# A GpSimd wait for the split row maxima, and a channel sum placed behind a gate remainder, in a four-block kernel on one core

## The chip, the cores and the metric

The kernel runs on one core of a Trainium2 chip. The metric is the device time of one execution in microseconds (us), the median of several runs. The engines are TensorE (PE in the profile; its weight loads are PEld), VectorE (DVE), ScalarE (ACT), GpSimd (POOL) and SyncE (SP, whose queue issues the DMAs). They run side by side, each its own instructions strictly in order, and wait for one another through semaphores.

## The reference, cut to what matters

Input x is 16 sequences of 512 tokens and 128 channels, fp32. Four blocks follow one another, each with a residual and a layer norm:

```
x = _layernorm(x + _L0_attn_ref(x, ...))   # time mix with a decaying sum, then channel mix
x = _layernorm(x + _L0_ffn_ref(x, ...))    # soft decision tree, depth 8
x = _layernorm(x + _L1_attn_ref(x, ...))   # causal attention, 16 heads of 8
x = _layernorm(x + _L1_ffn_ref(x, ...))    # 16 experts, the best 2 by softmax, plus 2 shared

# time mix:
k = exp(min(xk @ Wk, 60)); v = xv @ Wv; r = xr @ Wr
wk, wkv = _wkv(k, k * v, decay, first)     # running sums over the tokens
rwkv = sigmoid(r) * (wkv / (wk + 1e-8))
x = x + rwkv @ Wo
# channel mix:
kv = silu(xk @ cm_Wk) @ cm_Wv
x = x + (sigmoid(xr @ cm_Wr) + kv)
# attention: weights = softmax(causal scores)
# experts: g = softmax(u @ centroids.T + bias), kept for the 2 largest of 16
```

## The kernel before, in words

One sequence (a "batch" in the code, b = 0 to 15) goes through all four blocks as a [128 x 512] tile set. The work of five consecutive batches is interleaved. `run` (in `build`) counts turns; a table `ORDER` gives for each engine a list of tokens such as `1:gated0`, and in turn t the token `lag:step` runs that step for batch t - lag, if there is such a batch. So a list is the exact order of an engine's instructions, written out by hand. In the middle of the run every turn does one batch's worth of everything: lag 0 and 1 are the time and channel mix, lag 1 and 2 the tree and the making of q and k, lag 2 and 3 the attention, lag 3 and 4 the experts.

Semaphores count finished steps. `until(engine, b, name, n)` lets the engine wait until step `name` of batch b has been signalled n times (all its times if n is left out), and does nothing for a negative b.

The 512 hidden channels of the time mix are four chunks, c = 0 to 3. The steps that matter here, with their lines:

- `wk0` (L381, GpSimd): the first term is added to the decaying key sum of chunk 0. [128 x 512]
- `inverse0` (L675, VectorE): its reciprocal.
- `r_sig0` (L385, GpSimd): the sigmoid, from a tanh that ScalarE has made.
- `gated0` (L390, GpSimd): sigmoid times the decaying key-value sum of chunk 0. [128 x 512], both inputs in SBUF.
- `rwkv0` (L395, GpSimd): gated0 times inverse0. It needs both.
- `u15` (L436, GpSimd): the input of expert 15, of the batch that is three behind the time mix's; TensorE's `expert15` (L905, `wexpT`) needs it. GpSimd's list has it directly behind `gated0`.
- `max_parts` (L733, L638, L737, L739, VectorE): the row maxima of the attention scores, [128 x 64], are negated and split into three bf16 parts, by four small instructions, each of which waits for the one before. They signal `max_part` four times. TensorE's `maxT` (L905, `max_cols`) transposes the parts; its list goes on with experts 12 to 15, then `r2` and the scores (L905, `qh,kh`), which have the maxima as extra rows by way of a ScalarE copy and a DMA.
- `cmr_sig` (L403, GpSimd) and `cmr_sum` (L408, GpSimd): the channel mix's gate, and the gate plus the residual, [128 x 512].
- `y0` (L694, VectorE): that sum plus the channel mix's matmul. It needs `cmr_sum` and all of `cmv_ps`. Behind it VectorE's list has row maxima 8 and 9 and the statistics of y0, and TensorE's `xnT` waits for it.
- `largest0`, `others`, `largest1`, `gates` (L784 to L802, VectorE): the choice of two experts by small [128 x 64] instructions; `others` is the one that writes `left`.
- `gate_hi` and `gate_mid` (L488, ScalarE), `gate_rest` (L426, GpSimd) and `gate_lo` (L430, GpSimd): the gates split into three bf16 parts. gate_rest needs gate_hi, gate_mid needs gate_rest, gate_lo needs gate_mid. TensorE's `gT` needs gate_hi and gate_lo.

`max_parts` is at lag 3 in VectorE's list and `gated0` at lag 1 in GpSimd's, so in one turn they belong to batches two apart. In GpSimd's list `gated0` stands after `r_sig0` and `wk0`, and in VectorE's list `wkv0`, which it needs, stands eight steps ahead of `max_parts`.

Of the kernel before, what the change touches and what calls it, by code (L numbers as in the profile page):

```python
# [53 lines left out]
    pool="""  # L54
        4:u3 4:u5 4:u7 4:u9 4:u11 4:u13 1:r_sig0 1:wk0 1:gated0 4:u15 1:r_sig1 1:rwkv0 4:root7 1:wk1 1:gated1 0:root0 2:root_rms 1:r_sig2 1:gated2 1:rwkv1
        1:wk2 2:root4 1:wk3 2:rope_sum0 1:r_sig3 2:rope_sum1 2:rest0 1:gated3 1:rwkv2 1:rwkv3 2:part_lo0 2:rest1 2:part_lo1 1:res 1:root2 0:x1_gain
        0:x1_bias 0:root1 3:root6 1:cmr_sig 1:cmr_sum 3:gate_rest 3:gate_lo 1:root3 3:u1
    """,
    act="""
        4:route_exp 2:cmk_tanh3 2:cmr_tanh 1:norm1 4:gate_hi 4:gate_mid 1:mix_before0 4:gT_out 1:mix_before1 1:mix_before2 4:spread1 2:norm3 4:spread3  # L60
# [33 lines left out]
def build(nc: bass.Bass, a, out):  # L94
    with ExitStack() as ctx:
        def sb(name, shape, dt=F32):
            return ctx.enter_context(nc.sbuf_tensor(name, shape, dt))
# [6 lines left out]
        def raised(ins, name, by=1):  # L104
            ins.then_inc(sems[name], by)

        def until(eng, b, name, n=None):

            per = PER_BATCH[name]
            if b >= 0:  # L110
                eng.wait_ge(sems[name], b * per + (per if n is None else n))
# [74 lines left out]
        max_part, gate_part = (t[:, 0:J * PARTS * NH].rearrange("p (j i h) -> p j i h", j=J, i=PARTS) for t in (max_cols, gate_cols))  # L186
# [12 lines left out]
        gate_rest = sb("gate_rest", [P, J, NE])  # L199
# [135 lines left out]
        def _(pool):  # L335
# [51 lines left out]
            def gated(b, c):  # L387
                until(pool, b, "r_sig", c + 1)
                until(pool, b, "wkv", c + 1)
                raised(pool.tensor_tensor(rth[:, c % 2, :], rth[:, c % 2, :], kvb[:, c % 2, :], ALU.mult), "gated")  # L390

            def weighted(b, c):
# [39 lines left out]
            def gated_input(b, e):  # L432
# [5 lines left out]
            pool_steps = {  # L438
                **{f"root{n}": (lambda b, n=n: root(b, n)) for n in LNS}, "root_rms": root_rms, "x1_gain": first_gain, "x1_bias": first_bias,
                **each("wk", C, weight_sum), **each("r_sig", C, receptance), **each("gated", C, gated), **each("rwkv", C, weighted),  # L440
                "res": residual, "cmr_sig": channel_gate, "cmr_sum": channel_sum,
                **each("rope_sum", 2, rope_sum), **each("rest", 2, first_rest), **each("part_lo", 2, third_part),
# [794 lines left out]
```

How the kernel before makes its waits and increments, by code:

```python
        def until(eng, b, name, n=None):  # L107
            per = PER_BATCH[name]
            if b >= 0:
                eng.wait_ge(sems[name], b * per + (per if n is None else n))
# [1 line left out]
        def reached(eng, name, total):  # L113
            if total > 0:
                eng.wait_ge(sems[name], total)
# [177 lines left out]
        @block.sync  # L294
# [21 lines left out]
                until(sp, b, "out_ready")  # L316
                sp.dma_start(out[b].rearrange("(j p) h -> p j h", p=P), yo[:, :, :]).then_inc(sems["stored"], 16)
            load(0)
            for dst, src in GAINS:
                sp.dma_start(dst, src, allow_slow_non_contiguous=True).then_inc(setup["gains_in"], 16)
            for dst, src in FIRST[0::2]:
                sp.dma_start(dst, src, allow_slow_non_contiguous=True).then_inc(setup["first_loaded"], 16)
            for dst, src in LOADS[ON_ACT:]:
                sp.dma_start(dst, src, allow_slow_non_contiguous=True).then_inc(setup["loaded"], 16)
            sp.wait_ge(setup["bias_parts"], 7)
            for i in range(PARTS):
                sp.dma_start(bias_rows[i:i + 1, :], bias_part[i]).then_inc(setup["bias_in"], 16)
            sp.wait_ge(setup["kh_ones"], 4)
# [4 lines left out]
        @block.gpsimd  # L334
# [110 lines left out]
            ones_of_heads(0)  # L445
            ones_of_heads(1)
            pool.wait_ge(setup["constants"], 4)
            pool_steps["root0"](0)
            ones_of_heads(2)
            pool.wait_ge(setup["gains_in"], ALL_GAINS)
            pool_steps["x1_gain"](0)
            pool_steps["x1_bias"](0)
```

## Time and profile before

| | |
|---|---|
| median of 3 runs | 1956.96 us (1956.66 to 1959.65) |
| the profiled execution, own time | 1953.77 us |
| its span, first to last instruction | 1951.9 us |
| busy: PE, DVE | 1677.3 us (86%), 1554.8 us (80%) |
| busy: ACT, POOL | 1009.0 us (52%), 889.5 us (46%) |
| mean granted TensorE clock | 0.962 |
| chain that ended last, by engine | PE 49%, DVE 33%, POOL 6%, ACT 5% |

The span holds 20 turns, of which the 13 from turn 4 to turn 16 have all five batches in work; each of these takes about 110 us. "Busy" counts an instruction's time on its engine, waiting for the memory included. The chain is followed back from the last instruction, at each step to what released it. TensorE and VectorE take turns in bounding the program, so each stretch has to be read by itself.

### The profile page before, as it was taken

What the parts mean: (1) busy time and instruction counts of PE and PEld (TensorE: products, weight loads), DVE (VectorE), ACT (ScalarE), POOL (GpSimd) and SP (SyncE); (2) the same over time, 40 slices, a digit from 0 to 9 for tenths busy, and PEclk for the clock granted to TensorE, in tenths of its full rate; (3) what the DMA queues carried; (4) which work ended last, traced back from release to release, by engine and by line L of the source; (5) the groups of instructions that cost most, each with busy time, mean ns of one, the idle gap of its engine ahead of it and who ended that gap; (6) DMA issues with size and microseconds to landing.
All of it is one profiled execution on the core that took longest, in us unless ns stands there. A gap on an engine that the chain in (4) does not pass through costs nothing.

```text
span 1951.9 us, 34254 instructions
## 1 busy us (share of the span) xinstructions
PE 1677.3 (86%) x12161; PEld 1088.7 (56%) x12269; DVE 1554.8 (80%) x3386; ACT 1009.0 (52%) x1998; POOL 889.5 (46%) x1120
## 2 busy tenths in 40 slices
PE   3466898999899998999998998999998998988876
PEld 1234456565656656565655656565665656565634
DVE  4676879798897979798897979799897979793712
ACT  3233463737455463737556473836556473726152
POOL 4544253736355463727355463726345363622202
PEclk9687899999999999999999999999999999999897
DMA  3001010100102010100102010110102020100100
GB/s 98 0 6 54 2 53 5 45 16 18 45 3 60 2 55 7 38 24 14 49 2 60 2 55 8 33 29 10 53 2 61 2 55 1 31 26 22 35 7 6
DMA packets 66924, 53.39 MB, mean 27 GB/s; under 512 B 8322, under 2 KB 65474, under 8 KB 66754
## 3 DMA queue, kind: packets, MB, share of 16 engines
q1 hardware_dynamic: 63202, 49.55, 9.2%
q8 instruction: 98, 1.61, 0.4%
q10 hardware_dynamic: 3552, 1.65, 0.3%
q14 instruction: 72, 0.59, 0.1%
HBM read 8.44 MB, written 4.19 MB: 6 GB/s over the span
## 4 chain that ended last, share of the span: by engine, by line
PE 49%; DVE 33%; POOL 6%; ACT 5%; issue 5%; SPq 1%; DMA 0%; ACTq 0%; DVEq 0%; POOLq 0%; another core or an unknown queue 0%
PE bank L905 47%; DVE rmax L728 10%; PE bank L901 3%; DVE prob L808 3%; DVE stats L629 3%; ACT prob L488 2%; DVE rmax L725 2%; DVE mixed L638 2%; POOL rstd L351 2%; ACT xd L494 1%; DVE mv L634 1%; DVE kvsum L667 1%; SPq L325 1%; DVE left L638 1%; POOL x L399 1%
## 5 line engine op out<-in xcount | busy, mean ns | idle before, releaser
L488 ACT ACTIVATE prob<-bank 128x512 f32<-128x512 f32 x640 | 357.4, 597 | 95.5 <-PE bank L905 88.4
L728 DVE TENSOR_REDUCE rmax<-bank 128x1 f32<-128x512 f32 (+2 forms) x768 | 353.7, 502 | 14.6 <-PE bank L905 13.1
L436 POOL TENSOR_TENSOR prob<-xdT,spread 128x512 f32<-128x512 f32 x128 | 162.2, 1267 | 354.6 <-ACT spread L488 354.6
L905 PE MATMUL bank<-kh,qh 72*128 72x512 bf16 (+3 forms) x1024 | 266.6, 308 | 45.2 <-DVE rmax L728 36.3
L905 PE MATMUL bank<-wexpT,prob 128*128 128x128 f32 x2048 | 278.1, 284 | 0.8 <-POOL prob L436 0.6
L905 PE MATMUL bank<-qh,kh 75*128 75x512 bf16 (+3 forms) x1024 | 256.5, 304 | 20.6 <-ACT prob L488 17.8
L905 PEld LDWEIGHTS bank<-wexpT,prob 128*128 128x128 f32 x2048 | 259.9, 198 | 19.0 <-issue 12.5
L488 ACT ACTIVATE spread<-bank 128x512 f32<-128x512 f32 x128 | 76.4, 597 | 338.2 <-PE bank L905 330.1
L905 PEld LDWEIGHTS bank<-qh,kh 75*128 75x128 bf16 x1024 | 100.1, 98 | 206.9 <-ACT prob L488 138.2
L675 DVE RECIPROCAL wkb<-wkb 128x512 f32<-128x512 f32 x64 | 211.5, 3325 | 0.0
L905 PE MATMUL bank<-maskb,identb 128*128 128x128 bf16 x1024 | 194.4, 223 | 0.0
L905 PE MATMUL bank<-maskTb,identb 128*128 128x128 bf16 x1024 | 193.3, 221 | 0.0
L905 PEld LDWEIGHTS bank<-kh,qh 72*128 72x128 bf16 x1024 | 101.6, 99 | 143.5 <-DVE rmax L728 93.2
L905 PE MATMUL bank<-prob,vaug 128*32 128x512 f32 (+3 forms) x2048 | 176.2, 445 | 3.0 <-ACT prob L488 2.9
L347 POOL TENSOR_TENSOR var<-mv,eps_ln 128x4 f32<-128x4 f32 x112 | 27.7, 247 | 230.8 <-DVE mv L634 230.2
L905 PEld LDWEIGHTS bank<-maskb,identb 128*128 128x128 bf16 x1024 | 102.4, 100 | 39.0 <-issue 23.5
L381 POOL TENSOR_TENSOR wkb<-wkb,ksum 128x512 f32<-128x512 f32 x64 | 93.6, 1463 | 64.7 <-DVE ksum L662 56.5
L905 PEld LDWEIGHTS bank<-maskTb,identb 128*128 128x128 bf16 x1024 | 101.3, 99 | 24.2 <-issue 22.6
L351 POOL TENSOR_TENSOR rstd<-var,exponent 128x4 f32<-128x4 f32 x112 | 113.8, 1016 | 1.2
L488 ACT ACTIVATE rth<-bank 128x512 f32<-128x512 f32 x128 | 75.4, 589 | 68.4 <-PE bank L905 60.8
L395 POOL TENSOR_TENSOR inner<-rth,wkb 128x512 f32<-128x512 f32 x64 | 82.4, 1287 | 56.9 <-DVE wkb L675 55.3
L808 DVE TENSOR_TENSOR prob<-xdT,bank 128x512 f32<-128x512 f32 x128 | 86.9, 679 | 26.0 <-PE bank L905 22.4
(211 smaller groups left out, 3447.3 us busy)
## 6 DMA issues: line engine op xcount, KB each, us to landing
qh<-part SPq DMA_DIRECT2D x288, 64.0 KB
kh<-part SPq DMA_DIRECT2D x288, 64.0 KB
x<-in_L_attn_x_dram SPq DMA_DIRECT2D x16, 256.0 KB, 2.8
out_dram<-yo SPq DMA_DIRECT2D x16, 256.0 KB, 2.4
qh<-maxT SPq DMA_DIRECT2D x16, 48.0 KB
wk<-in_L_attn_tm_Wk_dram ACTq DMA_DIRECT2D x1, 256.0 KB
wv<-in_L_attn_tm_Wv_dram ACTq DMA_DIRECT2D x1, 256.0 KB
wr<-in_L_attn_tm_Wr_dram ACTq DMA_DIRECT2D x1, 256.0 KB
```

Of the source, the lines that this page charges most:

```text
L351: raised(pool.tensor_tensor(rstd[:, n, :], var[:, n, :], exponent[:, :], ALU.pow), f"root{n}")
L381: raised(pool.tensor_tensor(wkb[:, c % 2, :], wkb[:, c % 2, :], ksum[:, c % 2, 0:T], ALU.add), "wk")
L395: raised(pool.tensor_tensor(inner[:, c, :], rth[:, c % 2, :], wkb[:, c % 2, :], ALU.mult), "rwkv")
L436: raised(pool.tensor_tensor(ug[:, e % 4, :], xdT[:, :], spread[e // 2 % 2][:, :], ALU.mult), "ug_side")
L488: raised(act.activation(dst, src, func, **kw), signal)
L629: last = dve.bn_stats(stats[:, n, j, :], t[:, j, :])
L638: return dve.scalar_tensor_tensor(out=out_, in0=in0, scalar=scalar, in1=in1, op0=op0, op1=op1)
L675: raised(dve.reciprocal(wkb[:, c % 2, :], wkb[:, c % 2, :]), "wk_inv")
L728: last = dve.tensor_reduce(rmax[:, j, h:h + 1], S[n % 2][:, col:col + (j + 1) * P], AX_X, ALU.max)
L808: raised(dve.tensor_tensor(ug[:, e % 4, :], xdT[:, :], G, ALU.mult), "ug")
L901: last = pe.transpose(bk[:, j * P:(j + 1) * P], t[:, j, :], ident[:, :])
L905: return pe.matmul(out_, w, x, start=start, stop=stop, **kw)
```

## The change

Two edits. GpSimd's `gated0` of batch b additionally waits until `max_parts` of batch b - 2 has signalled all four times, which is the `max_parts` of the same turn. And GpSimd's list has `gate_rest` ahead of `cmr_sum` instead of behind it. No instruction is added or removed, and no other engine's list changes.

```diff
@@ -54,7 +54,7 @@
     pool="""
...
-        0:x1_bias 0:root1 3:root6 1:cmr_sig 1:cmr_sum 3:gate_rest 3:gate_lo 1:root3 3:u1
+        0:x1_bias 0:root1 3:root6 1:cmr_sig 3:gate_rest 1:cmr_sum 3:gate_lo 1:root3 3:u1
     """,
@@ -387,6 +387,8 @@
             def gated(b, c):
                 until(pool, b, "r_sig", c + 1)
                 until(pool, b, "wkv", c + 1)
+                if c == 0:
+                    until(pool, b - 2, "max_part")
                 raised(pool.tensor_tensor(rth[:, c % 2, :], rth[:, c % 2, :], kvb[:, c % 2, :], ALU.mult), "gated")
```

The first place, on GpSimd around `gated0` in a turn of the middle (`prob<-xdT,spread` are the experts' inputs, the last of them u15), before:

```order
L436 TENSOR_TENSOR prob<-xdT,spread 128x512 [waits s_expert_ps,s_spread_out] x5
L385 TENSOR_SCALAR rth<-rth 128x512 [waits s_r_tanh]
L381 TENSOR_TENSOR wkb<-wkb,ksum 128x512 [waits s_k_sum,s_k_first]
L390 TENSOR_TENSOR rth<-rth,kvb 128x512 [waits s_wkv,s_r_sig]
L436 TENSOR_TENSOR prob<-xdT,spread 128x512 [waits s_expert_ps,s_spread_out]
L385 TENSOR_SCALAR rth<-rth 128x512 [waits s_r_tanh]
L395 TENSOR_TENSOR inner<-rth,wkb 128x512 [waits s_wk_inv,s_gated]
```

The same place of the changed kernel:

```order
L438 TENSOR_TENSOR prob<-xdT,spread 128x512 [waits s_expert_ps,s_spread_out] x5
L385 TENSOR_SCALAR rth<-rth 128x512 [waits s_r_tanh]
L381 TENSOR_TENSOR wkb<-wkb,ksum 128x512 [waits s_k_sum,s_k_first]
L392 TENSOR_TENSOR rth<-rth,kvb 128x512 [waits s_max_part,s_wkv,s_r_sig]
L438 TENSOR_TENSOR prob<-xdT,spread 128x512 [waits s_expert_ps,s_spread_out]
L385 TENSOR_SCALAR rth<-rth 128x512 [waits s_r_tanh]
L397 TENSOR_TENSOR inner<-rth,wkb 128x512 [waits s_wk_inv,s_gated]
```

The order is the same (lines behind the edit read two higher); the product of `gated0` has one more semaphore to wait for, and u15, r_sig1 and rwkv0 are queued behind it.

The second place, on GpSimd between the gate of the channel mix and the last part of the expert gates, before:

```order
L355 TENSOR_TENSOR shift<-minus,rstd 128x4 [waits s_root6]
L403 TENSOR_SCALAR thr<-thr 128x512 [waits s_cmr_tanh]
L408 TENSOR_TENSOR thr<-thr,x_0 128x512 [waits s_res,s_cmr_sig]
L426 TENSOR_TENSOR gate_rest<-gts,gate_cols 128x64 [waits s_gate_hi]
L430 TENSOR_TENSOR gate_cols<-gate_rest,gate_cols 128x4x16 [waits s_gate_mid]
```

The same place of the changed kernel:

```order
L355 TENSOR_TENSOR shift<-minus,rstd 128x4 [waits s_root6]
L405 TENSOR_SCALAR thr<-thr 128x512 [waits s_cmr_tanh]
L428 TENSOR_TENSOR gate_rest<-gts,gate_cols 128x64 [waits s_gate_hi]
L410 TENSOR_TENSOR thr<-thr,x_0 128x512 [waits s_res,s_cmr_sig]
L432 TENSOR_TENSOR gate_cols<-gate_rest,gate_cols 128x4x16 [waits s_gate_mid]
```

The channel sum now stands behind the gates' remainder, and so behind the wait for ScalarE's gate_hi.

## Rows read from the trace of the kernel before

**Rows 1.** Chain that ended last, us 659.6 to 673, shares by line

```profile
by line: PE bank L905 66.8%; DVE max_rest L638 9.1%; DVE max_cols L737 8.7%; DVE rmax L725 4.5%; ACT prob L488 4.5%; DVE max_cols L739 4.3%; DVE max_cols L733 3.4%; issue 1.9%; PE bank L901 0.9%; ACTq L111 0.1%
```

**Rows 2.** Timeline, DVE: start us, us, engine, line, instruction

```profile
659.66 0.45 DVE L733 TENSOR_SCALAR max_cols<-rmax 128x64 bf16<-128x64 f32 x1
660.15 1.22 DVE L638 SCALAR_TENSOR_TENSOR max_rest<-rmax,max_cols 128x64 f32<-128x64 f32 x1
661.40 1.16 DVE L737 CAST max_cols<-max_rest 128x64 bf16<-128x64 f32 x1
662.59 0.57 DVE L739 TENSOR_TENSOR max_cols<-max_rest,max_cols 128x64 bf16<-128x64 f32 x1
663.08 3.34 DVE L675 RECIPROCAL wkb<-wkb 128x512 f32<-128x512 f32 x1
```

**Rows 3.** Timeline, POOL, the same stretch (wk0, gated0, u15, r_sig1)

```profile
658.79 1.27 POOL L381 TENSOR_TENSOR wkb<-wkb,ksum 128x512 f32<-128x512 f32 x1
660.01 1.27 POOL L390 TENSOR_TENSOR rth<-rth,kvb 128x512 f32<-128x512 f32 x1
661.23 1.27 POOL L436 TENSOR_TENSOR prob<-xdT,spread 128x512 f32<-128x512 f32 x1
662.46 0.63 POOL L385 TENSOR_SCALAR rth<-rth 128x512 f32<-128x512 f32 x1
```

**Rows 4.** Timeline, PE, the same stretch; in brackets idle before, and releaser

```profile
659.32 1.02 PE L905 MATMUL bank<-mixed,wk 128*128 128x512 f32 x2
663.22 0.40 PE L905 MATMUL bank<-identb,max_cols 128*128 128x128 bf16 x4 [2.88 <-DVE max_cols L739]
663.45 3.79 PE L905 MATMUL bank<-wexpT,prob 128*128 128x128 f32 x32
```

**Rows 5.** Instructions on max_cols, DVE: duration ns min/median/max, first and last start

```profile
L733 DVE TENSOR_SCALAR max_cols<-rmax x16: 194/454/459, 219.6 to 1855.1; 128x64 bf16<-128x64 f32 x16
L638 DVE SCALAR_TENSOR_TENSOR max_rest<-rmax,max_cols x16: 224/1216/1218, 219.8 to 1855.3; 128x64 f32<-128x64 f32 x16
L737 DVE CAST max_cols<-max_rest x16: 194/1154/1156, 220.1 to 1855.6; 128x64 bf16<-128x64 f32 x16
L739 DVE TENSOR_TENSOR max_cols<-max_rest,max_cols x16: 225/570/1218, 220.3 to 1855.8; 128x64 bf16<-128x64 f32 x16
```

**Rows 6.** Timeline, DVE: the reciprocal of chunk 1, same turn

```profile
681.84 3.32 DVE L675 RECIPROCAL wkb<-wkb 128x512 f32<-128x512 f32 x1
```

**Rows 7.** Timeline, POOL: a gated product begun beside it

```profile
684.38 1.28 POOL L390 TENSOR_TENSOR rth<-rth,kvb 128x512 f32<-128x512 f32 x1
```

**Rows 8.** Windows of one turn: length, busy (x) by engine PE to POOL, clock, DMA

```profile
438.24:549.74 111.50, 102.17 (x759) 67.46 (x765) 96.65 (x210) 62.27 (x124) 54.71 (x69) 0.98 0.10 28
549.74:659.66 109.92, 100.58 (x759) 65.78 (x765) 96.67 (x209) 62.18 (x124) 54.69 (x69) 1.00 0.10 28
```

**Rows 9.** Windows, two us behind TensorE's wait for max_cols in that first turn

```profile
444.00:446.00 2.00, 2.00 (x11) 2.00 (x11) 2.00 (x3) 0.42 (x1) 0.85 (x1) 0.50 0.09 25
```

**Rows 10.** Timeline, PE: experts 12 to 15 in the turn of rows 9

```profile
442.03 5.42 PE L905 MATMUL bank<-wexpT,prob 128*128 128x128 f32 x32
```

**Rows 11.** Chain that ended last, us 727 to 757, shares by line

```profile
by line: DVE rmax L728 40.9%; DVE prob L808 10.2%; issue 8.8%; DVE rmax L725 6.0%; DVE stats L629 5.5%; DVE mixed L638 5.4%; DVE left L638 4.5%; DVE kvsum L667 3.8%; DVE hot L792 2.6%; DVE tree L638 2.6%; DVE mv L634 2.3%; DVE kvb L657 2.0%
```

**Rows 12.** Instructions on left: duration ns min/median/max, first and last start us

```profile
L638 DVE SCALAR_TENSOR_TENSOR left<-hot,pe_ x16: 224/1332/1335, 286.1 to 1914.3; 128x64 f32<-128x64 f32 x16
```

**Rows 13.** Timeline, DVE: the end of gates, and y0

```profile
730.82 0.22 DVE L802 TENSOR_TENSOR gts<-pe_,hots 128x64 f32<-128x64 f32 x1
...
731.56 0.68 DVE L694 TENSOR_TENSOR x<-thr,bank 128x512 f32<-128x512 f32 x1
```

**Rows 14.** Timeline, POOL: cmr_sum and gate_rest

```profile
727.35 1.27 POOL L408 TENSOR_TENSOR thr<-thr,x 128x512 f32<-128x512 f32 x1
731.41 0.30 POOL L426 TENSOR_TENSOR gate_rest<-gts,gate_cols 128x64 f32<-128x64 f32 x1 [2.79 <-ACT gate_cols L488]
```

**Rows 15.** Timeline, ACT: gate_hi

```profile
731.08 0.26 ACT L488 ACTIVATE gate_cols<-gts 128x64 bf16<-128x64 f32 x1 [2.98 <-DVE gts L802]
```

## The prediction

> **What bounds the kernel now.** I began with the shares of busy time: TensorE 86% and VectorE 80%, neither full, so the bound moves between them within a turn. The chain of waits then says where. Around the split of the row maxima [rows 1] two thirds of the chain are TensorE's matmuls, but a quarter is the four small VectorE instructions of max_parts (9.1 + 8.7 + 4.3 + 3.4%). TensorE stands still for 2.88 us until the last of them is done [rows 4]. Around the choice of experts and the 25 us behind it the chain lies on VectorE nearly throughout [rows 11]. So what shortens max_parts moves the end, and what delays y0 moves it too. GpSimd is on neither path by its own work.
>
> **How long max_parts has to take.** Its four pieces took 0.45, 1.22, 1.16 and 0.57 us, 659.66 to 663.16 [rows 2]: 3.50 us. The instructions by name show the same four at their fastest: 0.194, 0.224, 0.194 and 0.225 us [rows 5]. The slow ones end in step with GpSimd. The first ends at 660.11, as wk0 does (660.06); the second at 661.37, as gated0 does (661.28); the third at 662.56, as u15 does (662.50); the fourth at 663.16, as r_sig1 does (663.09) [rows 2, 3]. A VectorE piece that is issued while a GpSimd instruction runs is thus held until that one ends. Medians near the slow values say that this is the rule: it is so in turns 4 to 16, 13 of the 16. The first split, in turn 3, is undisturbed, and the last two are disturbed in their last piece alone, by u15, with no gated0 about.
>
> **Part one, the wait of gated0.** It takes gated0, u15 and r_sig1, all behind it in GpSimd's order, out of this stretch. wk0 stays.
> - The first piece still runs beside wk0. Its price lies between 0.20 us (free) and 0.46 us (held). I take 0.45, as now, since wk0 ends at 660.06 in either kernel.
> - The other three run free, with the 0.03 us between them that they have now: 660.15 to 660.37, 660.40 to 660.59, 660.62 to 660.85. The end comes 663.16 - 660.85 = 2.3 us earlier.
> - TensorE's previous matmul ends at 660.34 [rows 4], so it can follow: its idle time falls from 2.88 to about 0.6 us. It issues maxT at 660.91, then experts 12 to 15.
> - gated0 starts 0.07 us after the last piece, the time GpSimd takes from ScalarE's gate_hi (731.34) to gate_rest (731.41) [rows 14, 15]: 660.92. u15 begins 1.23 us later and ends at 663.4. TensorE wants it for the last quarter of the 3.65 us of experts: 660.91 + 0.23 + 2.74 = 663.9. It is in time by 0.4 us. r_sig1 ends at 664.0, and rwkv0 needs the reciprocal, which begins at 660.78 and ends at 664.1. So nothing queued behind the wait is late, and there is no GpSimd DMA among it. ScalarE, SyncE's maxima transfer and VectorE's next clamp hang on events that all move 2.3 us forward.
> - New neighbours: gated0 and u15 now run beside the reciprocal instead of beside the small pieces. Such a pair stands in the trace: a gated product of 1.28 us begins in the middle of a reciprocal of 3.32 us [rows 6, 7], and neither is longer than elsewhere (1.27 and 3.34). I cost it at nothing. By the Trainium skill (SBUF — State Buffer, "Who interferes with whom") VectorE and GpSimd share one pair of memory ports; whoever issues first keeps it for the whole instruction, and copy, cast and tensor_scalar can take it with a single SBUF input. The reciprocal is not in that list; were it treated like those, rival 2 would be what happens.
>
> Sum of part one: 13 turns x 2.3 = 29.9 us less.
>
> **The clock behind it.** In some turns TensorE's granted clock falls to 0.50, its 1.2 GHz level, directly behind the 2.88 us of standing still [rows 9], and experts 12 to 15 take 5.42 instead of 3.79 us [rows 4, 10]. Such a turn lasts 111.5 instead of 109.9 us [rows 8]; one turn of each kind is shown, and of the 13 four are of the slow kind. In the whole middle of the program the clock falls nowhere else. With 0.6 us of standing still I expect the four falls to go: 4 x 1.6 = 6.4 us less, with ends of 0 and 6.4.
>
> **Part two, the channel sum behind gate_rest.** cmr_sum, 727.35 to 728.62, now holds up the piece that writes left (1.33 instead of 0.22 us) [rows 12, 14]. Away from there it frees VectorE's choice of experts by 1.11 us. But VectorE then comes to y0, and y0 needs cmr_sum. Step by step: gates end at 731.04 - 1.11 = 729.93 [rows 13]; gate_hi starts 0.04 later and ends at 730.23; gate_rest runs 730.30 to 730.60; cmr_sum starts 0.04 before that end and takes 1.27: 731.83; y0 starts 0.05 later, at 731.88. Before, it started at 731.56. So VectorE gains 1.1 us, waits for all of it and 0.3 us more. gate_lo moves from 732.38 to about 732.1 and holds nobody. Since this stretch is VectorE's [rows 11], the 0.3 us counts, in the 14 turns (3 to 16) in which gates and channel sum meet: 4.5 us more. Its ends: 0, if TensorE's row maxima absorb it, and 14 x 0.6 = 8.4, if each handover costs a little more.
>
> **Sum.** 1953.8 (the profiled execution's own time; span 1951.9) - 29.9 - 6.4 + 4.5 = 1922.0 us. The median of the runs is 3.2 us above the profiled execution. If that is two more falls of the clock it goes as well, if not it stays: 1922 to 1925. I say 1923.
>
> **Rivals.**
> 1. *The clock still falls*, as often as now, elsewhere in the turn: TensorE would now stand about 1 us in one piece where it waits for y0. Then 1953.8 - 29.9 + 4.5 = 1928, 1931 by the median. Against it: all four falls followed the long wait. Chance 0.20. Experts kept waiting for u15 (its 0.4 us used up, say 0.2 us late) end in the same place: 13 x 0.2 = 2.6 us, 1926; within the forecast's range.
> 2. *The reciprocal holds up gated0 (slower).* It is issued at 660.78, before gated0. If GpSimd had to wait for its end at 664.1, u15 would end at 664.1 + 1.23 + 1.27 = 666.6, and expert 15, due at 663.9, would start 2.7 us late: more than the 2.3 us gained. 13 x 0.4 = 5 us more, the clock as now, and part two's 4.5: 1957.0 + 10 = 1967. It decides from 2.3 us of delay on. Rows 6 and 7 speak against it. Chance 0.03.
> 3. *The change doesn't do what it says:* the small pieces are slow for a reason of their own, and moving GpSimd frees none. Then part one gives 0 (the 0.6 us left of u15's and rwkv0's slack still cover it), and y0 waits for gate_rest at its old end, 731.71, plus 1.23 for the sum and 0.05: 732.99, 1.43 us late. 14 x 1.43 = 20 us: 1977. The undisturbed 0.2 us in turns without these neighbours [rows 5, 12] speak against it. Chance 0.03.
> 4. *Part two costs nothing* because VectorE makes good its 0.3 us behind y0, and the falls go too: 1918. Chance 0.12.
>
> **Numbers.** The forecast has 0.62, its own range 1919 to 1928. The range given reaches from just below rival 4 to rival 1 by the median, 1916 to 1932, and leaves out rivals 2 and 3 and the unforeseen. A difference of 0.2%, 3.9 us, is about what measurements of this kernel can tell from none. Faster by more than that: the forecast, rivals 1 and 4, 0.94; slower: rivals 2 and 3, with some chance that either is milder than worked out, 0.04; within: 0.02.
>
> **What would show it.** In the changed profile: pieces two to four of max_parts at 0.19 to 0.23 us in all 16 turns, the first still 0.45; TensorE's idle time ahead of maxT near 0.6 us; gated0 starting within 0.1 us behind the last piece; experts 12 to 15 at about 3.8 us without a gap, in every turn; turns of about 107.9 us; left at 0.22 us; VectorE idle for 1.4 us ahead of y0, released by GpSimd; y0 0.3 us later counted from the logits' first instruction. It would be wrong if VectorE's reciprocal or GpSimd's product grew beside each other, if TensorE waited for u15, or if the clock fell in more turns than four.

## The result, and the profile after

The changed kernel takes 1933.9 us (median of 4 runs, 1932.13 to 1935.45); the kernel before, on the same chip, 1957.07. The ratio is 0.9878 with a 95% interval of 0.9862 to 0.9893: 23 us faster. The forecast was 1923 with a range of 1916 to 1932, so the gain was a third smaller than said, and the time lies just outside the range. Of all the executions behind this document one, of the kernel with part one alone, took 4075 us; its ratio leaves it out.

The page of the changed kernel, busy time, and the chain that ended last:

```profile
PE 1684.5 (87%) x12161; PEld 1092.2 (57%) x12269; DVE 1512.3 (78%) x3386; ACT 1008.8 (52%) x1998; POOL 888.4 (46%) x1120
...
PE 53%; DVE 26%; POOL 7%; issue 7%; ACT 5%; SPq 1%; DMA 0%; DVEq 0%; ACTq 0%; POOLq 0%; another core or an unknown queue 0%
```

VectorE lost 42 us of "busy" time though it has the same 3386 instructions: that was time in which small instructions were held, 13 x 2.3 us in max_parts and 14 x 1.1 us in `left`, less 3 us by which the row maxima grew. Its share of the chain fell from 33% to 26%. TensorE's busy time grew by 7 us with the same instructions, which is the first sign of its clock.

**The first place.** Timelines of the changed kernel around max_parts, VectorE, GpSimd and TensorE:

```profile
653.87 0.46 DVE L735 TENSOR_SCALAR max_cols<-rmax 128x64 bf16<-128x64 f32 x1
654.36 0.23 DVE L640 SCALAR_TENSOR_TENSOR max_rest<-rmax,max_cols 128x64 f32<-128x64 f32 x1
654.62 0.20 DVE L739 CAST max_cols<-max_rest 128x64 bf16<-128x64 f32 x1
654.85 0.22 DVE L741 TENSOR_TENSOR max_cols<-max_rest,max_cols 128x64 bf16<-128x64 f32 x1
654.99 3.34 DVE L677 RECIPROCAL wkb<-wkb 128x512 f32<-128x512 f32 x1
...
655.25 1.27 POOL L392 TENSOR_TENSOR rth<-rth,kvb 128x512 f32<-128x512 f32 x1 [0.97 <-DVE max_cols L741]
656.47 1.27 POOL L438 TENSOR_TENSOR prob<-xdT,spread 128x512 f32<-128x512 f32 x1
...
655.13 0.40 PE L907 MATMUL bank<-identb,max_cols 128*128 128x128 bf16 x4 [0.58 <-DVE max_cols L741]
655.37 3.79 PE L907 MATMUL bank<-wexpT,prob 128*128 128x128 f32 x32
```

They answer to [rows 2 to 4]. Pieces two to four take what they take alone; all four need 1.20 us instead of 3.50. TensorE's standing still fell from 2.88 to 0.58 us. gated0 and u15 run beside the reciprocal, and neither is longer. The experts run through, 3.79 us.

**The second place.** VectorE's last gate instruction and y0, GpSimd's gate_rest and channel sum, and TensorE's xnT:

```profile
613.60 0.23 DVE L804 TENSOR_TENSOR gts<-pe_,hots 128x64 f32<-128x64 f32 x1
...
615.83 0.69 DVE L696 TENSOR_TENSOR x<-thr,bank 128x512 f32<-128x512 f32 x1 [1.40 <-POOL thr L410]
...
614.20 0.31 POOL L428 TENSOR_TENSOR gate_rest<-gts,gate_cols 128x64 f32<-128x64 f32 x1 [3.05 <-ACT gate_cols L490]
614.46 1.26 POOL L410 TENSOR_TENSOR thr<-thr,x 128x512 f32<-128x512 f32 x1
...
616.67 0.63 PE L903 MATMUL bank<-ident,hat 128*128 128x128 f32 x4 [1.24 <-DVE x L696]
```

The table of waits sums it up over the run:

```profile
DVE x L696 <- POOL thr L410: 20.0, 14, 1.8
```

In 14 turns VectorE waits 20.0 us for the channel sum, which it never did before. And TensorE, which in the kernel before had no wait here longer than about half a microsecond, stands still for 1.24 us in one piece.

**The clock.** Windows of a turn, of the next one, two us in that turn, and from turn 16's max_parts to the end (columns as in [rows 8]):

```profile
545.84:653.87 108.03, 100.61 (x759) 65.72 (x765) 93.39 (x209) 62.17 (x124) 54.65 (x69) 1.00 0.10 28
653.87:763.69 109.82, 103.00 (x759) 67.85 (x765) 93.67 (x210) 62.18 (x124) 54.68 (x69) 0.97 0.10 28
...
728.00:730.00 2.00, 2.00 (x18) 1.80 (x17) 2.00 (x5) 0.00 (x0) 0.59 (x2) 0.50 0.00 0
...
1630.42:1931.70 301.28, 249.49 (x1871) 163.06 (x1885) 155.54 (x384) 132.58 (x259) 88.10 (x111) 0.90 0.07 21
```

A turn at full clock takes 108.03 us; 109.92 before [rows 8]. But the clock still falls to 0.50, in six turns instead of four, and no longer behind maxT: five times within 2 to 4 us behind the wait ahead of xnT, and once, in turn 16, at the same place without an xnT, since no batch follows. Three of the six falls last twice as long, 6.8 instead of 3.4 us. In the profiled executions the 20.2 us between the spans come about so: 12 turns (from turn 4's max_parts to turn 16's) x 1.89 = 22.7 less; what else makes them differ, the falls first, 5.8 before and 5.3 now, 0.6 less with rounding; the start 0.5 more; the stretch from turn 16's max_parts to the end 301.3 instead of 298.7, 2.6 more. A short fall behind xnT lengthens its turn by 0.6 us and a long one by 1.8, where one behind maxT cost 1.6, so the five falls of the middle turns cost no more than the four before. The loss lies at the end: turn 16 has a fall of 6.8 us where it had none and takes 105.92 us, where part one alone gives 103.20; from there to the end it is 195.4 us instead of 193.2.

### The profile page after: what moved, and what is told of

It is laid out like the page before. It is cut to its first block, busy times and chain, and to the rows that moved or that the text cites. A ratio compares the mean times of both kernels' runs of the same rounds, so it can differ in the third digit from the quotient of the medians.

```text
span 1931.7 us, 34254 instructions
## 1 busy us (share of the span) xinstructions
PE 1684.5 (87%) x12161; PEld 1092.2 (57%) x12269; DVE 1512.3 (78%) x3386; ACT 1008.8 (52%) x1998; POOL 888.4 (46%) x1120
## 3 DMA queue, kind: packets, MB, share of 16 engines
HBM read 8.44 MB, written 4.19 MB: 7 GB/s over the span
## 4 chain that ended last, share of the span: by engine, by line
PE 53%; DVE 26%; POOL 7%; issue 7%; ACT 5%; SPq 1%; DMA 0%; DVEq 0%; ACTq 0%; POOLq 0%; another core or an unknown queue 0%
PE bank L907 50%; DVE rmax L730 8%; PE bank L903 3%; DVE stats L631 3%; DVE prob L810 3%; ACT prob L490 2%; DVE rmax L727 2%; POOL rstd L351 2%; DVE mixed L640 2%; ACT xd L496 1%; DVE mv L636 1%; DVE kvsum L669 1%; SPq L325 1%; POOL x L401 1%; POOL thr L410 1%
## 5 line engine op out<-in xcount | busy, mean ns | idle before, releaser
L907 PE MATMUL bank<-kh,qh 72*128 72x512 bf16 (+3 forms) x1024 | 271.0, 312 | 33.7 <-DVE rmax L730 25.7
L907 PEld LDWEIGHTS bank<-wexpT,prob 128*128 128x128 f32 x2048 | 256.0, 195 | 19.2 <-issue 12.5
L392 POOL TENSOR_TENSOR rth<-rth,kvb 128x512 f32<-128x512 f32 x64 | 88.6, 1385 | 30.8 <-DVE max_cols L741 27.2
```

Of the source, the lines that this page charges most:

```text
L907: return pe.matmul(out_, w, x, start=start, stop=stop, **kw)
```

## The experiments

Ten further kernels, each timed against the kernel before on its own chip (1955.7 to 1957.4). "Falls" below are those of turns 4 to 16, counted in the one profiled execution of each kernel; the times are medians of all.

**1. Each part alone.** Theory A: the clock falls where TensorE stands still longest, so part two brought the falls back. Rival B: the falls come at their own rate, whatever is waited for.

```diff
-        1:cmr_sig 3:gate_rest 1:cmr_sum 3:gate_lo
+        1:cmr_sig 1:cmr_sum 3:gate_rest 3:gate_lo
```

> The changed kernel with GpSimd's list as it was: channel sum ahead of the gates' remainder, the wait of gated0 kept. Theory A (the clock falls where TensorE stands still longest in one piece; in the changed kernel that is the 1.24 us ahead of xnT, which part two made): y0 no longer waits, the piece ahead of xnT is gone, the six falls of turns 4 to 16 go. From 1933.9: 14 x 0.33 = 4.6 us for y0 and 5 to 8 us for the clock, 1921 to 1924. Rival B (the clock falls about as often whatever TensorE waits for, for instance since it rests less and works more densely): only the 4.6 us, about 1929, with falls still in the middle turns.

Measured: 1919.4 us, ratio 0.9807 (0.9790 to 0.9823); the executions took 1917.9, 1919.2, 1919.6 and 4075 us. A turn, the 12 turns, and the end:

```profile
545.33:652.97 107.64, 100.95 (x766) 65.78 (x765) 94.39 (x209) 62.18 (x124) 54.76 (x69) 1.00 0.10 29
330.04:1621.33 1291.29, 1211.47 (x9181) 789.91 (x9180) 1131.88 (x2501) 746.33 (x1477) 657.08 (x817) 1.00 0.10 28
1621.33:1917.40 296.07, 245.31 (x1887) 158.68 (x1885) 156.41 (x384) 132.42 (x259) 88.19 (x111) 0.92 0.08 21
```

Part one alone beats both kernels. Every turn is like the next: not one fall. So part two costs 14.5 us on top of part one: 0.39 us in each turn by itself, and the rest through the clock, in the middle (5.7 us) and at the end (301.3 against 296.1), less 1.2 us by which the start differs. B is out.

The other way about, the kernel before with part two alone:

```diff
-        1:cmr_sig 1:cmr_sum 3:gate_rest 3:gate_lo
+        1:cmr_sig 3:gate_rest 1:cmr_sum 3:gate_lo
```

> The kernel before with the gates' remainder ahead of the channel sum, and no new wait. Theory A: y0 0.33 us late in 14 turns (4.6 us), and the clock now falls in two places, behind the 2.9 us ahead of maxT and behind the 1.2 us ahead of xnT: 1957 + 4.6 + 5 to 8 = 1967 to 1970. Rival B: 1957 + 4.6 = 1962, falls as often as before. A third outcome, 1957 or less, would say that y0's delay is absorbed.

Measured: 1971.3 us, ratio 1.0073 (1.0056 to 1.0091). Part two by itself is slower than doing nothing. A turn with a fall, one without, two us of a fall, and xnT:

```profile
553.34:665.28 111.94, 102.59 (x766) 67.37 (x765) 95.70 (x210) 62.33 (x124) 54.68 (x69) 0.98 0.10 27
665.28:775.63 110.35, 101.01 (x766) 65.72 (x765) 95.71 (x210) 62.24 (x124) 54.67 (x69) 1.00 0.10 28
...
558.00:560.00 2.00, 2.00 (x12) 2.00 (x11) 2.00 (x1) 0.00 (x0) 0.00 (x0) 0.50 0.06 15
...
738.42 0.63 PE L901 MATMUL bank<-ident,hat 128*128 128x128 f32 x4 [1.24 <-DVE x L694]
```

The time is 1.3 us above A's range, but it does not come about as A says: A had falls in both places. The undisturbed turn is 0.43 us longer, and there are eight falls instead of four, all of them behind maxT. Behind xnT, where TensorE waits the same 1.24 us, there is none. So the length of a wait does not decide by itself.

**2. Filling the waits.** Dummy matmuls that nobody waits for, in the changed kernel ahead of xnT, in the kernel before ahead of maxT.

```diff
-        3:busy_gates1 0:xnT
+        3:busy_gates1 3:busy_gates2 3:busy_gates0 0:xnT
```

> The changed kernel with four more dummy matmuls of TensorE, 0.22 us each, in the 1.24 us that it stands still ahead of xnT. Nothing waits for them. Theory A: the falls behind xnT go or become rare, 1926 to 1929. Rival B: 1934, falls as before.

Measured: 1927.7 us, ratio 0.9853 (0.9838 to 0.9867). xnT in this kernel, and 5.95 us around it, here and then in the changed kernel:

```profile
724.68 0.63 PE L903 MATMUL bank<-ident,hat 128*128 128x128 f32 x4 [0.38 <-DVE x L696]
...
722.00:727.95 5.95, 4.62 (x34) 2.42 (x32) 4.51 (x16) 2.97 (x6) 2.68 (x6) 1.00 0.15 44
```

```profile
722.00:727.95 5.95, 3.79 (x27) 1.96 (x26) 4.51 (x15) 2.97 (x6) 2.67 (x6) 0.91 0.17 44
```

The other engines do the same in both, and y0 waits 1.40 us for the channel sum in either; TensorE is busy for 4.62 us instead of 3.79. The falls of turns 4 to 15 are gone (one is left, in turn 16, where there is no xnT any more) and 6.2 us with them.

```diff
-        0:k2 2:maxT
+        0:k2 2:busy_maxima0 2:busy_maxima1 2:busy_maxima2 2:maxT
```

> The kernel before with six dummy matmuls, 0.22 us each, in the 2.88 us that TensorE stands still ahead of maxT. Theory A: the four falls there go, 6 us less: 1951. Rival B: 1957, falls as before.

Measured: 1949.3 us, ratio 0.9960 (0.9950 to 0.9970), no fall. maxT, and the 12 turns:

```profile
664.52 0.40 PE L905 MATMUL bank<-identb,max_cols 128*128 128x128 bf16 x4 [1.46 <-DVE max_cols L739]
...
331.06:1650.21 1319.15, 1228.63 (x9253) 795.90 (x9252) 1159.61 (x2500) 746.89 (x1477) 657.32 (x817) 1.00 0.10 28
```

1319.15 us instead of 1324.87 for the same turns: the four falls cost 5.7 us. (The nine executions took 1946.6 to 1952.9 us. The profiled one is the slowest: its start and its end are together 4.9 us longer than in the profiled execution of the kernel before, and hide most of the gain.) A wait of 1.46 us is left here, longer than the 1.24 us that the changed kernel has ahead of xnT, and nothing falls behind it.

**3. Where the falls go.** Part two alone again, with the stretch ahead of maxT filled, and then with both filled.

> Run e2_order_only with the six dummy matmuls of e4_fill_maxT ahead of maxT. In e2_order_only all eight falls of turns 4 to 16 lay behind maxT and none behind xnT, though TensorE stands 1.24 us there as in the changed kernel. Theory C (in a turn the clock falls behind its emptiest stretch; once the one ahead of maxT is filled, the one ahead of xnT is it): the falls move behind xnT, five or more of them, 1964 to 1969. Rival D (the 1.24 us alone bring no fall; the changed kernel's falls there need something else of its own): no falls in the middle, 1949.3 + 5.6 = 1955.

Measured: 1961.1 us (1960.9 to 1967.1), ratio 1.0035 (1.0021 to 1.0049). xnT, the windows around one of the falls, and the emptiest 6 us at maxT and at xnT:

```profile
739.70 0.63 PE L901 MATMUL bank<-ident,hat 128*128 128x128 f32 x4 [1.24 <-DVE x L694]
...
850.00:852.00 2.00, 1.65 (x15) 1.08 (x15) 1.97 (x8) 1.32 (x3) 0.00 (x0) 1.00 0.33 100
852.00:854.00 2.00, 1.43 (x9) 0.86 (x9) 2.00 (x8) 1.26 (x2) 1.52 (x4) 0.59 0.14 39
854.00:856.00 2.00, 2.00 (x15) 1.51 (x14) 1.78 (x4) 0.00 (x0) 0.00 (x1) 0.50 0.00 0
...
664.10:670.10 6.00, 4.54 (x28) 2.58 (x27) 5.57 (x10) 2.01 (x4) 5.91 (x6) 1.00 0.00 0
738.50:744.50 6.00, 3.75 (x34) 2.37 (x35) 5.60 (x18) 2.62 (x5) 2.04 (x6) 1.00 0.16 44
```

The falls have moved: six in turns 4 to 15, all behind xnT, every second one long, as in the changed kernel, and a seventh in turn 16 at the same place. TensorE is now busy for 4.54 of the emptiest 6 us at maxT and for 3.75 of those at xnT; in the kernel with part two alone it was 3.15 and 3.75. The median is 3 us below what C gave. The executions differ by up to 6 us; the profiled one is the slowest of them, 1967.1.

> The same with the four dummy matmuls ahead of xnT as well. Theory C: no falls in turns 4 to 15, 1955 to 1957. Rival D: the same as e9_order_fill_maxT within 1 us. If falls stay behind xnT here, neither holds.

Measured: 1955.5 us, ratio 1.0003 (0.9993 to 1.0012), with one fall left, behind xnT. C fits these runs with that one exception: the clock falls behind the stretch of a turn in which TensorE is least busy, and when that stretch is filled or shortened, the falls may go to the next emptiest. C says where, and not how often: part two leaves the emptiest stretch as it was, at maxT, and the falls there go from four to eight. What makes the clock fall in one turn and not in the next was not tried, so that part is not shown.

**4. How much slack u15 has.** Part one with u15 behind r_sig1.

```diff
-        1:gated0 4:u15 1:r_sig1
+        1:gated0 1:r_sig1 4:u15
```

> Part one with u15 moved behind r_sig1, 0.6 us later. It tests the slack of u15. In e1_wait_only u15 ends at 656.84 and TensorE wants it at about 657.2, so it would now end at 657.45, 0.25 us late. Theory (TensorE is the bound there, slack 0.4 us): 13 x 0.25 to 0.35 = 3 to 5 us, 1923 to 1924. Rival (the next bound there is VectorE's reciprocal and clamp ahead of r2, at the same time as the experts' end, so that TensorE has slack of its own): 1919 to 1920.

Measured: 1922.1 us, ratio 0.9827 (0.9811 to 0.9843). The time lies between the two forecasts, but this kernel and the next three ran on a chip on which the kernel before takes 1955.7 us, 1.7 less than where part one alone was timed. By the ratios it is 3.9 us slower than part one alone, within the theory's 3 to 5. TensorE's experts 12 to 15, and the waits over the run:

```profile
654.24 4.19 PE L907 MATMUL bank<-wexpT,prob 128*128 128x128 f32 x32
...
PEld bank L907 <- POOL prob L438: 5.4, 15, 0.6
```

The experts take 4.19 instead of 3.79 us and the turn 108.00 instead of 107.64. The twelve turns are 4.3 us longer than with part one alone (1295.6 against 1291.3), and there is no fall in either. The slack was there and it was about as small as worked out.

**5. Better places.** The channel sum where it was, but waiting for the second hot vector, with row maxima 6 and 7 done meanwhile:

```diff
-        3:largest1 2:rowmax6 3:gates 2:rowmax7 1:y0
+        3:largest1 2:rowmax6 2:rowmax7 3:gates 1:y0
...
                 until(pool, b, "res")
+                until(pool, b - 2, "hot", 2)
```

> Part one (run e1_wait_only, 1919.4) and another place for the channel sum: ahead of gate_rest as before, but it waits for the second hot vector, and VectorE does row maxima 6 and 7, which read PSUM, right then, and the gates after them. Theory: GpSimd holds up only small VectorE work on SBUF; beside the row maxima the sum costs nothing and is done before y0 asks. VectorE's stretch is 1.0 to 1.1 us shorter per turn in 14 turns, turns of 106.6 us, 1905 us; up to 1911 if TensorE (row maxima 8 and 9, ready for it later than y0) takes part of it. Rival: the sum disturbs the row maxima as well (0.6 us or more in their durations), or y0 waits for it: 1919 or more.

Measured: 1905.7 us, ratio 0.9741 (0.9726 to 0.9756). The row maxima, gates and y0, the channel sum, and the turn:

```profile
610.19 1.34 DVE L731 TENSOR_REDUCE rmax<-bank 128x1 f32<-128x384 f32 x3
611.45 0.34 DVE L803 TENSOR_TENSOR hots<-hot 128x64 f32<-128x64 f32 x1
611.83 0.23 DVE L805 TENSOR_TENSOR gts<-pe_,hots 128x64 f32<-128x64 f32 x1
611.98 0.68 DVE L697 TENSOR_TENSOR x<-thr,bank 128x512 f32<-128x512 f32 x1
...
610.45 1.27 POOL L411 TENSOR_TENSOR thr<-thr,x 128x512 f32<-128x512 f32 x1 [1.79 <-DVE hot L795]
...
543.32:650.01 106.69, 100.44 (x759) 65.72 (x765) 93.46 (x210) 62.23 (x124) 54.83 (x69) 1.00 0.10 29
```

Three reductions from PSUM take 1.34 us beside the channel sum (0.55, 0.28 and 0.68, each as long as in the kernel with part one alone), and hots, a sum of two SBUF operands, is held for the 0.1 us that the sum still runs. y0 follows the gates without a wait in all turns but one (0.2 us). The Trainium skill (SBUF — State Buffer, "Who interferes with whom") says that a tensor_reduce never contends for the pair of ports that VectorE and GpSimd share and that an instruction with two SBUF inputs does. The trace agrees on both counts, 1.34 us for the reductions and 0.34 instead of 0.21 us for hots; the reductions here read PSUM, and none that reads SBUF ran beside the sum.

And u15 and the wait ahead of r_sig0 and gated0:

```diff
-        1:r_sig0 1:wk0 1:gated0 4:u15 1:r_sig1
+        1:wk0 4:u15 1:r_sig0 1:gated0 1:r_sig1
...
+                if e == NE - 1 and b + 1 < B:
+                    until(pool, b + 1, "max_part")
```

> Part one, rearranged: GpSimd's order is wk0, u15, r_sig0, gated0, and the wait for the split maxima stands on u15 (of the batch one older) instead of on gated0. All four pieces should be free (0.19 to 0.23 us), also in the last two turns with experts. Theory (a GpSimd instruction that runs when a small piece is issued holds it until it ends, and nothing else does): 0.25 us per turn in 13 turns and 1 us in each of the last two, 1919.4 - 5 = 1914. Rival: gated0 comes 0.6 us later and rwkv0, waited for by ScalarE, with it: the 5 us are given back, 1919.

Measured: 1916.5 us, ratio 0.9801 (0.9786 to 0.9816). Against part one alone that is 3 us by the medians, but 1.2 us by the ratios, whose intervals overlap: a gain smaller than the 5 us expected and not clear of noise. The four pieces by name, the start of the scores, and the turn:

```profile
L735 DVE TENSOR_SCALAR max_cols<-rmax x16: 194/195/195, 219.1 to 1819.6; 128x64 bf16<-128x64 f32 x16
L640 DVE SCALAR_TENSOR_TENSOR max_rest<-rmax,max_cols x16: 224/226/227, 219.3 to 1819.8; 128x64 f32<-128x64 f32 x16
L739 DVE CAST max_cols<-max_rest x16: 195/195/196, 219.6 to 1820.1; 128x64 bf16<-128x64 f32 x16
L741 DVE TENSOR_TENSOR max_cols<-max_rest,max_cols x16: 224/226/226, 219.8 to 1820.3; 128x64 bf16<-128x64 f32 x16
...
658.02 0.10 PEld L907 LDWEIGHTS bank<-qh,kh 75*128 75x128 bf16 x1 [0.81 <-DMA qh<-maxT]
...
544.54:652.10 107.56, 100.70 (x759) 65.70 (x765) 94.69 (x209) 62.32 (x124) 55.76 (x68) 1.00 0.10 29
```

All 64 pieces are free now, which shows the mechanism whole. But the turn is 0.08 us shorter, not 0.25: the scores start 4.92 us behind maxT instead of 4.76 and wait for the maxima's DMA, 0.81 us; with part one alone they waited 0.59 us for it. That transfer is the next bound there.

Both together:

> The two rearrangements of e5_sum_beside_rowmax and e6_u15_first together. They touch different stretches, so the gains should add: 1919.4 - 14 - 5 = 1900. Rival: if one turns TensorE into the bound of the whole turn, less than the sum, 1905 or more.

Measured: 1903.4 us, ratio 0.9737 (0.9722 to 0.9753). The time lies between the sum (1900) and the rival (1905). The median is 2.3 us below that of the first alone, but the executions overlap (1902.1 to 1907.4 against 1901.4 to 1906.4), so whether the second rearrangement adds anything to the first is not shown; in the traces a turn is 0.1 us shorter. Both versions are about 30 us below the changed kernel, the fastest found.

## Why the prediction was right, and where it failed

- *max_parts is held by GpSimd, 2.3 us per turn.* Right: 3.50 to 1.20 us, and part one alone gave 109.92 - 107.64 = 2.28 us per turn. The first piece stayed at 0.46.
- *Nothing behind the wait is late.* Right. gated0 starts 0.18 us behind the last piece, not 0.07, so u15's slack is 0.3 rather than 0.4 us; experiment 4 used it up.
- *The reciprocal and gated0 don't disturb each other.* Right; rival 2 is out, and so is rival 3, since left fell to 0.22 us too.
- *Part two, y0 0.3 us late.* Mechanism right, size a little low: 0.39 to 0.43 us per turn, because GpSimd begins gate_rest 0.08 and VectorE y0 0.11 us after what they wait for, where 0.07 and 0.05 were taken. With 14 turns that is 5.5 to 6 us instead of 4.5. It was not absorbed, so rival 4 is out.
- *The four falls go, 6.4 us.* This is the step that failed. They did go from behind maxT, as said, and six came at the other place, five behind xnT, where part two leaves TensorE standing 1.24 us, and one in turn 16. Part one alone has none, and with TensorE's wait ahead of xnT filled the five are gone. Rival 1 had named that place and 1 us of waiting there and got 0.20; it should have been the forecast. Even its 1928 to 1931 was too low by 3 us. It let the falls cost what they cost before, and in the middle turns they did not cost more; but one came in turn 16, where there was none, and the end of the program, which part one should have made 2 us shorter, took 2.6 us more. The sign named for it, the clock falling in more turns than four, is what came. The reasoning looked at where the clock had fallen and took that place for the cause. It was only the emptiest stretch of the turn, and the change emptied another one.

So of two edits one gained and one lost. Without part two the forecast's own sum, 29.9 + 6.4 us off 1957, would have come out at 1921; it measured 1919.

## What to carry to other kernels

A tiny VectorE instruction on the critical path can be held by a long GpSimd one until that ends; look for medians several times the minimum of the same instruction, and give the GpSimd work a wait that puts it beside reductions from PSUM or a reciprocal. Moving a producer behind a later wait frees what it disturbed, but look at who consumes it: here y0 lost more than the gates won. And when a wait of TensorE is shortened, list the emptiest stretches that remain in the period before counting the clock as won; a few dummy matmuls in the new one test it cheaply.

## What the runs showed of the hardware that was not expected

- The falls of the granted clock move. Filling 1.3 us of a 2.88 us wait removed all four (1957.4 to 1949.3 us); adding a 1.24 us wait elsewhere in the same turn doubled them at the old place (8 instead of 4), and filling the old place sent them to the new one (six there, and a seventh at the same place in turn 16).
- Falls behind xnT are alternately 3.4 and 6.8 us long in the two kernels that have several of them (the changed one, and part two with maxT filled; in the latter the seventh, of turn 16, is short again); those behind maxT are all 3.4 us, four in the kernel before and eight with part two alone. Why was not tried.
- In the changed kernel a GpSimd instruction that waits for VectorE starts 0.16 to 0.18 us after it (gated0 at 655.25 behind the last piece's end at 655.07, rwkv0 at 658.49 behind the reciprocal's at 658.33), one that waits for ScalarE 0.08 us (gate_rest at 614.20 behind gate_hi's end at 614.12).
